# One weighted pass over values and ones in the log attention, with picking matmuls and a re-cut order of the steps

## The chip, the cores and the metric

The kernel runs on one core of a Trainium2 chip. The metric is the time of one execution on the device in microseconds; lower is better. An interval between two kernels comes from runs of both on the same chip.

## What is computed

The input is x, 8 batches of 512 tokens with 128 features, all float32. Four layers follow each other, each added to x after a layer norm: a linear attention, a mixture of 8 experts with a shared one (two chosen per token), the *log attention*, and the mixture of experts again. The change touches the log attention:

```
qkv = x @ w_qkv.T ; k_y = x @ w_ky.T            # 16 heads of 8 dims
L   = q.k  * scale ; L_y = q.k_y * scale         # 512 x 512 per head
agg = sum(exp(clip(L_y, -15, 15)) * mask, -1) + EPS
r   = log(abs(L) + eps) - log(agg + eps)
w   = softplus(r) * mask
A   = w / (sum(w, -1) + EPS)
out = (A @ v) @ w_proj.T
```

So there are two passes over the scores of a batch. *A* makes exps of L_y and sums them. *B* makes the weights w and needs, for each query, the sum of w times the values (8 numbers a head, the numerators) and the sum of w (one number a head).

## The kernel before

Everything is written out by hand: each engine has its own program, and semaphores join them. In the log attention the work goes in steps. `tensor_step`, `scalar_step`, `vector_step` and `pool_step` are called for n = 0 to 99 (and early, for negative n, from inside the first experts' layer by `TENSOR_LEAD`, `VECTOR_LEAD`, `SCALAR_LEAD`). A batch has DUS = 10 steps; n = 10a + i, so i is the place in a batch's ten. Step n does the A part of unit n and the B part of unit m = n - 16 (LAG = 6 and ten steps). Steps 0 to 15 have A alone, 16 to 79 both, 80 to 95 B alone, and from 80 on the second experts' layer is led in (`lead_tensor`, `lead_vector`, `lead_pool`).

`PIECES` says what unit i covers: one or two (s, kb, column, q0, width), 512 columns in all, where s is one of four stacks of heads, kb a block of 128 keys and q0 the first query. A unit covers 4 heads (j). Each step has two halves, u = 0 and 1, of two heads each:

- TensorE (PE): `scores` of half 0 (L1735), `sum_exps` (L1767, exps of unit n - 2 times `ones_s` into bank 4), `weight_values(.., 5)` (L1783, weights of unit m - 2 times `values` into bank 5), `scores` of half 1, `weight_values(.., 6)` (L1783 too, the same weights times `ones_s` into bank 6), then one extra of the batch's ten.
- VectorE (DVE): `abs_scores` half 0 (L2001, out of PSUM), `clip_exps` of the last step's half 1 (L1993), `abs_scores` half 1, extras, `clip_exps` half 0, extras.
- ScalarE (ACT): `exponential` half 0 (L1875), `logarithm` (L1881), extras, `exponential` half 1, `logarithm`, extras.
- GpSimd (POOL): the masks (L2112), and indirect DMAs of the experts' layers around it.

A's scores have banks 0 and 1, B's have 2 and 3, in steps 16 to 79. So half 1 of `scores` can start when exp and abs of half 0 have read these banks, and the next half 0 when those of half 1 have.

A weights matrix of 32 columns for stack s has values in 8 columns (8s to 8s+7) and zeros elsewhere, so the four stacks add up side by side in one bank. The ones matrices are built alike.

The extras of a batch on PE, each at a step's end: `project` q again for r (q2, i = 0), `project_out` (1), `turn` (2), `project` q, ky, k (3, 4, 5), `project_v` (6), `sum_prefix` in three parts (7 to 9). All of them use bank 7, one after the other in the order of `SHARED_BANK`: each waits until ACT or DVE has read the one before. On DVE `empty` (L2045, L2046) reads banks 6 and 5 at i = 8, `correct` (L2035, L2036) makes two corrections at i = 9, `divide` (L2051) follows at 9, `split_low` (L2008) makes low parts of q, ky, k at 4 to 6. `add_choice` (L1483) adds results of the first experts' layer at i = 0 and 1 of a ten, up to a = 5, so in four of the tens within steps 16 to 79. ACT makes the high parts (`split_high`, L1891) and `copy_v` (L1902), and inverts with Ln and Exp.

Below are the functions that the diff touches.

## Time and profile before

| | us |
|---|---|
| median of 3 runs | 1060.55 (1060.13 to 1067.85) |
| the profiled execution | 1063.56 |
| its span, first to last instruction | 1061.8 |
| PE busy | 855.8 |
| DVE busy | 732.6 |
| ACT busy | 566.2 |
| POOL busy | 569.9 |

A span is one execution seen by the profiler; what lies outside it (1.8 us) is the launch and the end. Busy is the union of an engine's instructions; matmuls overlap each other, so a busy PE need not be at its peak. One fp32 matmul of the program makes two records of PE. In the rows, PEld is the weight load of PE; `x_res` rows named in the log attention are `r_buf` and `d_buf`, `w_a` is `q_scaled`, `y_out` is `delta_v` and `delta_n`, `ring_a` is the exps and `ring_b` the weights.

### The profile page before, as it was taken

The page shows a single profiled execution, that of the slowest core. Times are in us where ns is not written, and L with a number is a line of the kernel's source. Part 1 is how long each engine was busy: PE and PEld are TensorE (multiplying, and loading weights), DVE is VectorE, ACT ScalarE, POOL GpSimd, SP SyncE. Part 2 cuts the span into 40 slices and gives each one's busy share as a digit, 9 for nine tenths or more (in the row PEclk, how much of TensorE's full clock was granted, in tenths as well). Part 3 has the DMA queues.
Part 4 walks back from the last instruction along what each step waited for, and adds up shares of the span by engine and source line. Part 5 has one row for each costly group of instructions (what it writes and reads, how often), then busy time and mean ns, then how long its engine had stood idle before and what let it go on. Part 6 is the DMA issues. An engine that isn't in the chain of part 4 may idle for free.

```text
span 1061.8 us, 21386 instructions
## 1 busy us (share of the span) xinstructions
PE 855.8 (81%) x7419; PEld 571.3 (54%) x7419; DVE 732.6 (69%) x1538; ACT 566.2 (53%) x797; POOL 569.9 (54%) x774
## 2 busy tenths in 40 slices
PE   4887577899986778888888888888888767899890
PEld 2676466799872333333333333343444346799890
DVE  3888746465654578797978787778878835465574
ACT  2454242233345778797878788778773332233230
POOL 2343685870655565556533333334324887788784
PEclk9999688999996899999999999999987788999896
DMA  9970012142355766555637363732210021132444
GB/s 298 271 103 1 20 40 70 61 129 81 98 150 157 215 188 186 160 153 151 190 103 197 88 207 93 209 87 77 80 41 11 31 78 40 39 91 81 137 124 128
DMA packets 114120, 123.85 MB, mean 117 GB/s; under 512 B 13296, under 2 KB 76272, under 8 KB 113888
## 3 DMA queue, kind: packets, MB, share of 16 engines
q1 hardware_dynamic: 96224, 100.54, 34.1%
q0 software_dynamic: 8416, 17.29, 5.2%
q10 hardware_dynamic: 9376, 4.65, 1.5%
q8 instruction: 63, 1.03, 0.4%
q14 instruction: 41, 0.34, 0.1%
HBM read 59.71 MB, written 62.72 MB: 115 GB/s over the span
## 4 chain that ended last, share of the span: by engine, by line
PE 41%; DVE 17%; issue 14%; POOL 13%; ACT 6%; DMA 5%; SPq 2%; POOLq 0%; DVEq 0%; ACTq 0%
PE psum L1783 7%; PE psum L1735 6%; DVE ring_b L2001 5%; PE psum L1767 5%; PE psum L828 4%; POOL y_token L1065 4%; POOL pause_room L486 3%; POOL x_sorted L1041 3%; PE psum L1801 2%; PE psum L842 2%; PE psum L780 2%; DVE parts L2008 2%; PE psum L791 2%; PE psum L751 2%; PE psum L1816 1%
## 5 line engine op out<-in xcount | busy, mean ns | idle before, releaser
L2001 DVE TENSOR_SCALAR ring_b<-psum 128x1024 int32<-128x1024 int32 x160 | 195.0, 1222 | 71.7 <-PE psum L1735 71.3
L1875 ACT ACTIVATE ring_a<-psum 128x1024 f32<-128x1024 f32 x160 | 163.2, 1024 | 88.3 <-PE psum L1735 82.2
L2112 POOL TENSOR_SCALAR_AFFINE_SELECT ring_b<-ring_b 128x512 f32<-128x512 f32 (+1 forms) x112 | 84.6, 770 | 215.3 <-ACT ring_b L1881 215.1
L1881 ACT ACTIVATE ring_b<-ring_b 128x1024 f32<-128x1024 f32 x160 | 168.3, 1053 | 41.0 <-DVE ring_b L2001 40.6
L1735 PE MATMUL psum<-stacks 32*128 32x128 f32 (+3 forms) x1024 | 102.9, 387 | 40.4 <-DVE ring_b L2001 22.0
L1993 DVE TENSOR_SCALAR ring_a<-ring_a 128x1024 f32<-128x1024 f32 x160 | 120.4, 757 | 21.5 <-ACT ring_a L1875 21.4
L1735 PEld LDWEIGHTS psum<-stacks 32*128 32x128 f32 x1024 | 59.4, 193 | 132.2 <-issue 73.3
L943 ACT ACTIVATE ring_b<-psum 128x512 f32<-128x512 f32 x72 | 42.6, 591 | 111.5 <-PE psum L828 79.5
L1783 PE MATMUL psum<-ring_b,values 128*32 128x256 f32 (+3 forms) x1024 | 91.5, 467 | 9.1 <-POOL ring_b L2112 5.6
L2112 POOL TENSOR_SCALAR_AFFINE_SELECT ring_a<-ring_a 128x512 f32<-128x512 f32 (+1 forms) x112 | 81.1, 737 | 27.9 <-DVE ring_a L1993 27.9
L1767 PE MATMUL psum<-ring_a,ones_s 128*32 128x256 f32 (+3 forms) x1024 | 93.2, 474 | 2.5 <-POOL ring_a L2112 1.5
L1086 POOL DMA_INDIRECT r_rows<-y_sorted,rows_of x64 | 68.8, 1075 | 48.8 <-issue 41.7
L842 PE MATMUL psum<-w_expert,ring_b 128*128 x568 | 85.3, 285 | 11.9 <-ACT y_out L959 7.0
L1439 DVE TENSOR_TENSOR ring_b<-psum,ring_b 128x512 f32<-128x512 f32 x72 | 49.2, 684 | 64.0 <-ACT ring_b L943 51.3
L1783 PE MATMUL psum<-ring_b,ones_s 128*32 128x256 f32 (+3 forms) x1024 | 91.2, 464 | 0.0
L842 PEld LDWEIGHTS psum<-w_expert,ring_b 128*128 128x128 f32 x568 | 72.8, 194 | 19.0 <-issue 18.9
L1065 POOL DMA_INDIRECT y_token<-y_out,token_of x71 | 70.9, 998 | 22.0 <-POOL pause_room L486 18.7
L1041 POOL DMA_INDIRECT x_sorted<-r_rows,rows_of x64 | 63.8, 996 | 31.3 <-POOL pause_room L486 15.3
L486 POOL MEMSET pause_room<- 128x256 f32 x220 | 75.9, 345 | 0.2
L1041 POOL DMA_INDIRECT x_marked<-r_rows,rows_of x64 | 63.8, 997 | 20.9 <-POOL pause_room L486 16.0
L828 PE MATMUL psum<-ring_a,ring_b 128*128 128x128 f32 x576 | 72.0, 279 | 3.5 <-issue 1.9
L828 PEld LDWEIGHTS psum<-ring_a,ring_b 128*128 128x128 f32 x576 | 69.0, 196 | 4.9 <-issue 3.0
(211 smaller groups left out, 1492.0 us busy)
## 6 DMA issues: line engine op xcount, KB each, us to landing
stack_q<-parts SPq DMA_DIRECT2D x32, 256.0 KB
stack_ky<-parts SPq DMA_DIRECT2D x32, 256.0 KB
stacks<-stack_q SPq DMA_DIRECT2D x64, 128.0 KB
stacks<-stack_ky SPq DMA_DIRECT2D x64, 128.0 KB
stack_k<-parts SPq DMA_DIRECT2D x32, 256.0 KB
stacks<-stack_k SPq DMA_DIRECT2D x64, 128.0 KB
stack_qr<-parts SPq DMA_DIRECT2D x32, 256.0 KB
stacks<-stack_qr SPq DMA_DIRECT2D x64, 128.0 KB
```

The costliest lines, as they stand in the source:

```text
L828: mm = nc.tensor.matmul(bank(2 * (k % 2) + g)[:, at:at + 128], w_pages[i % 4][:, g * INNER + c * 128:g * INNER + (c + 1) * 128], x_turned[ ...
L842: mm = nc.tensor.matmul(tiles(bank(4))[:, i % 4, :], hidden[:, self.items.index(("pair", j)) % 8, at:at + 128], w["w_expert"][:, bass.ds(s ...
L1041: nc.gpsimd.indirect_dma_start(out=out, out_offset=bass.IndirectOffsetOnAxis(ap=rows_of[:, n, at + t:at + t + 1], axis=0), in_=row, in_off ...
L1065: nc.gpsimd.indirect_dma_start(out=y_token, out_offset=bass.IndirectOffsetOnAxis(ap=token_of[:, n, s:s + 1], axis=0), in_=y_out[:, n % 2, ...
L1735: mm = nc.tensor.matmul(bank(2 * pair + j % 2)[:, column:column + width], keys[rows, s, kb * 128:(kb + 1) * 128], queries[rows, s, q0:q0 + ...
L1767: mm = nc.tensor.matmul(psum[32 * j:32 * j + 32, 4, q0:q0 + width], ones_s[:, s, :], exps[:, n % RING, j, column:column + width], start=i ...
L1783: mm = nc.tensor.matmul(psum[32 * j:32 * j + 32, into, q0:q0 + width], weight, ring[:, m % RING, j, column:column + width], start=i == 0, ...
L1875: nc.scalar.activation(exps[:, n % RING, 2 * u:2 * u + 2, :], psum[:, first:first + 2, :], ACT.Exp, scale=SCALE).then_inc(self.exp, 1)
L1881: nc.scalar.activation(part, part, ACT.Ln, bias=1.0).then_inc(self.ln, 1)
L1993: nc.vector.tensor_scalar(part, part, CLIP_LO, CLIP_HI, ALU.max, ALU.min).then_inc(self.clip, 1)
L2001: nc.vector.tensor_scalar(ring[:, m % RING, HEADS_B[u][0]:HEADS_B[u][1] + 1, :].bitcast(I32), psum[:, first:first + 2, :].bitcast(I32), 0x ...
L2112: ins = nc.gpsimd.affine_select(out=part, in_=part, pattern=[[0, part.ap[1][1]], [1, 128]], compare_op=ALU.is_ge, fill=0.0, base=0, channe ...
```

## The change

1. **One pass.** A weights matrix now has, for two neighbouring stacks, 16 columns each: 8 of values and 8 of ones. `weight_values` runs once a unit. Units 0 to 4 of a batch (stacks 0 and 1) add into bank 5, units 5 to 9 (stacks 2 and 3) into bank 6; `PIECES` is re-ordered for that. POOL writes the ones once, beside the memset of the values' room.
2. **Picks.** Numerators and sums now lie mixed in two banks. ACT copies bank 5 out (`evict_first`, i = 3), DVE bank 6 (`evict_second`, i = 8), and TensorE picks them apart by four fp32 matmuls of 128x512 a batch with 0/1 matrices: sums at i = 8 and 9, numerators at i = 0 of the next ten (for the last batch all four at once, at i = 8 and 9). `take_sums` and `take_numerators` read them from bank 6 in place of `empty`.
3. **Order.** The extras of PE now stand at two places of a step, after `sum_exps` and after `weight_values`, and neighbours use different banks: q2 and the picks bank 6, v and ky bank 5, the rest bank 7. DVE's and ACT's extras are placed anew too.

```diff
+    column = np.arange(D)
+    group, stack, dim = column // 32, column // HD % GROUPS, column % HD
+    for name, shift in (("pick_numerators", 0), ("pick_sums", HD)):
+        pick = np.zeros((128, 2, D))
+        pick[32 * group + 2 * HD * (stack % 2) + shift + dim, stack // 2, column] = 1
...
-        VECTOR_LEAD = {0: (-12,), 4: (-6,), 5: (-5,), 6: (-4, -7), 9: (-2,)}
-        TENSOR_LEAD = {3: (-8,), 4: (-7,), 5: (-6,), 6: (-5,)}
+        VECTOR_LEAD = {0: (-12,), 4: (-6,), 5: (-5,), 6: (-4, -3), 9: (-2,)}
+        TENSOR_LEAD = {3: (-7,), 4: (-6,), 5: (-5,), 6: (-4,)}
...
+                    ones = bass.AP(values, HD, [values[:].ap[0], [2 * OW, 2 * TT * HALF], [OW + 2 * HD, 2], [1, HD]])
+                    nc.gpsimd.memset(ones, 1.0).then_inc(set_values, 1)
...
+        BANK_OF = {"q2": 6, "v": 5, "ky": 5, "y": 7, "turn": 7, "q": 7, "k": 7, "prefix": 7}
...
-            def weight_values(self, pe, m, into):
+            def weight_values(self, pe, m):
...
+                pe.wait_ge(self.mask_b, m + 1)
+                if i == 0:
+                    pe.wait_ge(self.v_ready, b + 1)
+                    pe.wait_ge(self.first_out, b)
+                    pe.wait_ge(self.v_tok, min(b + 2, B))
...
+                if i == HALF_DONE:
+                    pe.wait_ge(self.emptied, 2 * b)
+                    pe.wait_ge(self.q_ready, min(b + 2, B))
+                into = 5 if i < HALF_DONE else 6
...
+            def pick(self, pe, b, n, a):
+
+                if n == 0 and a == 0:
+                    pe.wait_ge(self.first_out, b + 1)
+                    pe.wait_ge(self.second_out, b + 1)
+                if n == 1 and a == 0:
+                    pe.wait_ge(self.emptied, 2 * b + 1)
+                mm = nc.tensor.matmul(bank(6), picks[n][:, a, :], evicted[a], start=a == 0, stop=a == 1, skip_group_check=True)
...
                 self.scores(pe, n, m, 0)
                 if 0 <= n - 2 < STEPS_A:
                     self.sum_exps(pe, n - 2)
...
+                if i == 0 and 0 <= a - 3 < B - 1:
+                    self.pick(pe, a - 3, 1, 0)
+                if i == 2 and 0 <= a - 3 < B - 1:
+                    self.project_out(pe, a - 3)
+                if i == 3 and a + 1 < B:
+                    self.turn(pe, a + 1)
+                if i in (4, 5, 6) and a + 1 < B:
+                    self.project(pe, ("q", "ky", "k")[i - 4], a + 1)
+                if i in (7, 8) and 0 <= a - 1 < B:
+                    self.sum_prefix(pe, a - 1, ((0,), (2,))[i - 7])
+                if i == 9 and 0 <= a - 2 < B:
+                    if last:
+                        self.pick(pe, a - 2, 1, 0)
+                    self.pick(pe, a - 2, int(last), 1)
...
                 self.scores(pe, n, m, 1)
...
+                    self.weight_values(pe, m - 2)
+                if i == 0 and 0 <= a - 3 < B - 1:
+                    self.pick(pe, a - 3, 1, 1)
+                if i == 1 and 0 <= a - 1 < B:
                     self.project(pe, "q2", a - 1)
...
+                if i == 3 and 0 <= a < B:
                     self.project_v(pe, a)
...
+                if i == 8 and 0 <= a - 2 < B:
+                    self.pick(pe, a - 2, 0, 0)
+                    if last:
+                        self.pick(pe, a - 2, 0, 1)
...
+            def evict_first(self, a, b):
+                a.wait_ge(self.weighted, DUS * b + HALF_DONE)
...
+                nc.scalar.copy(evicted[0], bank(5)).then_inc(self.first_out, 1)
...
+            def evict_second(self, v, b):
                 v.wait_ge(self.weighted, DUS * (b + 1))
+                v.wait_ge(self.q_ready, min(b + 2, B))
+                nc.vector.tensor_copy(evicted[1], bank(6)).then_inc(self.second_out, 1)
```

In `scalar_step`, `invert_sums` goes to the end of i = 1, `finish_delta` to i = 8, `invert_weights` from i = 8 to i = 0 of the next ten (for the last batch it stays), `evict_first` and `copy_v` stand at i = 3 and 4 ahead of `exponential` half 1, and `split_high` behind it. In `vector_step`, `scale_q` goes from the end of i = 1 into i = 2, `add_output` from 2 to 3, `add_choice` from 0 and 1 to 4 and 5, the statistics from 3 to 7, the corrections to 0 and 1 of the next ten, and most extras stand between the two halves. `pool_step`'s rstd goes from 4 to 8.

PE, a middle step of a batch (i = 5), before: two halves of scores, the exps' sums, values, ones, and the projection k at the end.

```order
L1735 MATMUL psum<-stacks 128x256 x2
L1735 MATMUL psum<-stacks 128x512 x2
L1735 MATMUL psum<-stacks 128x256 x2
L1767 MATMUL psum<-ring_a,ones_s 32x384 x4
L1767 MATMUL psum<-ring_a,ones_s 32x128 x4
L1783 MATMUL psum<-ring_b,values 32x512 x4
L1735 MATMUL psum<-stacks 128x256 x2
L1735 MATMUL psum<-stacks 128x512 x2
L1735 MATMUL psum<-stacks 128x256 x2
L1783 MATMUL psum<-ring_b,ones_s 32x512 x4
L1801 MATMUL psum<-o_tok,b_k 128x512
```

The same step of PE now (L1762 is the scores, L1794 the exps' sums, L1815 the weights times values and ones, L1844 a projection):

```order
L1762 MATMUL psum<-stacks 128x512 x4
L1794 MATMUL psum<-ring_a,ones_s 32x384 x4
L1794 MATMUL psum<-ring_a,ones_s 32x128 x4
L1844 MATMUL psum<-o_tok,b_ky 128x512
L1762 MATMUL psum<-stacks 128x512 x4
L1815 MATMUL psum<-ring_b,values 32x256 x8
```

One pass of 512 columns by four heads is gone from the second half, and the projection (ky now) stands in the first.

PE at the end of a batch's B part now, i = 8 second half to i = 9 (L1828 is a pick, L1859 `sum_prefix`):

```order
L1762 MATMUL psum<-stacks 128x512 x2
L1762 MATMUL psum<-stacks 128x384 x2
L1762 MATMUL psum<-stacks 128x128 x2
L1794 MATMUL psum<-ring_a,ones_s 32x256 x8
L1828 MATMUL psum<-x_res,pick_sums 128x512
L1762 MATMUL psum<-stacks 128x512 x2
L1762 MATMUL psum<-stacks 128x384 x2
L1762 MATMUL psum<-stacks 128x128 x2
L1815 MATMUL psum<-ring_b,values 32x384 x4
L1815 MATMUL psum<-ring_b,values 32x128 x4
L1859 MATMUL psum<-reaches,v_tok 128x128
```

A pick stands where nothing but the values' pass stood before, in the first half of step i = 9; the last part of `sum_prefix` stays at its end.

DVE from `empty` in i = 8 to `divide` in i = 9, before (the corrections L2035 and L2036 follow right behind it):

```order
L2045 TENSOR_TENSOR x_res<-psum,y_out 128x512
L2046 TENSOR_TENSOR oT<-psum,y_out 128x512
L1993 TENSOR_SCALAR ring_a<-ring_a 128x1024
L2001 TENSOR_SCALAR ring_b<-psum 128x1024
L2027 COPY values<-v_tok 128x4x4x8 x4
L1987 SCALAR_TENSOR_TENSOR nbias<-mean_var,rstd 128x4
L1993 TENSOR_SCALAR ring_a<-ring_a 128x1024
L2001 TENSOR_SCALAR ring_b<-psum 128x1024
L1993 TENSOR_SCALAR ring_a<-ring_a 128x1024
L2001 TENSOR_SCALAR ring_b<-psum 128x1024
L1993 TENSOR_SCALAR ring_a<-ring_a 128x1024
L2051 TENSOR_TENSOR oT<-oT,x_res 128x512
```

and now, over both steps (L2067 abs, L2059 clip, L2115 `evict_second`, L2095 `copy_values`, L2123 `take_sums`):

```order
L2067 TENSOR_SCALAR ring_b<-psum 128x1024
L2059 TENSOR_SCALAR ring_a<-ring_a 128x1024
L2115 COPY x_res<-psum 128x512
L2067 TENSOR_SCALAR ring_b<-psum 128x1024
L2095 COPY values<-v_tok 128x8x2x8 x4
L2053 SCALAR_TENSOR_TENSOR nbias<-mean_var,rstd 128x4
L2059 TENSOR_SCALAR ring_a<-ring_a 128x1024
L2067 TENSOR_SCALAR ring_b<-psum 128x1024
L2059 TENSOR_SCALAR ring_a<-ring_a 128x1024
L2067 TENSOR_SCALAR ring_b<-psum 128x1024
L2123 TENSOR_TENSOR x_res<-psum,y_out 128x512
L2059 TENSOR_SCALAR ring_a<-ring_a 128x1024
```

Three operations of 512 columns and two corrections stood in these two steps, now two in all do; the others moved into the next ten.

## Rows read from the trace of the kernel before

**Rows 1.** Page, part 1: busy us (share of span) xinstructions of each engine.

```profile
PE 855.8 (81%) x7419; PEld 571.3 (54%) x7419; DVE 732.6 (69%) x1538; ACT 566.2 (53%) x797; POOL 569.9 (54%) x774
```

**Rows 2.** Windows: length, then busy and count of PE, PEld, DVE, ACT, POOL; clock; DMA; GB/s.

```profile
383.70:749.20 365.50, 309.88 (x3462) 138.91 (x3462) 300.17 (x422) 296.84 (x352) 162.38 (x210) 0.97 0.50 146
749.20:814.30 65.10, 54.88 (x447) 27.30 (x443) 52.42 (x140) 40.93 (x66) 17.31 (x22) 0.87 0.17 49
814.60:938.30 123.70, 97.97 (x659) 72.59 (x659) 75.56 (x182) 39.40 (x58) 98.96 (x150) 0.85 0.16 50
```

**Rows 3.** Groups of 400 to 800 us: count, busy, mean ns of one, idle before, releaser.

```profile
L2001 DVE TENSOR_SCALAR ring_b<-psum 128x1024 int32<-128x1024 int32 x139 | 169.8, 1222 | 65.5 <-PE psum L1735 65.1 <-issue 0.2
L1783 PE MATMUL psum<-ring_b,ones_s 128*32 128x384 f32 (+3 forms) x888 | 76.0, 449 | 0.0
L1783 PE MATMUL psum<-ring_b,values 128*32 128x384 f32 (+3 forms) x888 | 75.4, 448 | 3.5 <-DVE oT L2046 3.5
...
L1801 PE MATMUL psum<-o_tok,b_k 128*128 128x512 f32 x6 | 3.4, 644 | 2.8 <-DVE parts L2008 2.8
...
L2045 DVE TENSOR_TENSOR x_res<-psum,y_out 128x512 f32<-128x512 f32 x6 | 4.1, 681 | 0.0
```

**Rows 4.** Waits of 400 to 800 us: total, times, longest.

```profile
DVE ring_b L2001 <- PE psum L1735: 65.1, 99, 3.0
ACT ring_a L1875 <- PE psum L1735: 59.0, 68, 2.1
```

**Rows 5.** Timeline of one step (i = 5), and its first row a batch later: start, us.

```profile
551.17 0.51 PE L1735 MATMUL psum<-stacks 32*128 32x256 f32 x6
551.61 1.07 PE L1767 MATMUL psum<-ring_a,ones_s 128*32 128x384 f32 x16
551.72 1.23 DVE L2001 TENSOR_SCALAR ring_b<-psum 128x1024 int32<-128x1024 int32 x1 [1.06 <-PE psum L1735]
551.76 1.03 ACT L1875 ACTIVATE ring_a<-psum 128x1024 f32<-128x1024 f32 x1 [1.60 <-PE psum L1735]
...
552.86 0.68 DVE L1993 TENSOR_SCALAR ring_a<-ring_a 128x1024 f32<-128x1024 f32 x1
553.47 0.51 PE L1735 MATMUL psum<-stacks 32*128 32x256 f32 x6
...
554.02 1.23 DVE L2001 TENSOR_SCALAR ring_b<-psum 128x1024 int32<-128x1024 int32 x1 [0.48 <-PE psum L1735]
...
555.90 1.12 PE L1801 MATMUL psum<-o_tok,b_k 128*128 128x512 f32 x2 [0.93 <-DVE parts L2008]
...
610.09 1.23 DVE L2001 TENSOR_SCALAR ring_b<-psum 128x1024 int32<-128x1024 int32 x1 [1.06 <-PE psum L1735]
```

**Rows 6.** Windows around falls of the clock, columns as in rows 2.

```profile
344.00:350.00 6.00, 4.21 (x47) 1.94 (x39) 2.83 (x5) 4.56 (x6) 3.60 (x4) 1.00 0.70 217
...
588.00:592.00 4.00, 2.45 (x16) 2.04 (x14) 2.56 (x7) 3.44 (x5) 0.37 (x1) 0.73 0.00 0
...
776.00:781.00 5.00, 3.00 (x26) 1.73 (x22) 3.18 (x6) 3.49 (x6) 2.23 (x3) 1.00 0.00 0
...
816.00:821.00 5.00, 5.00 (x41) 2.01 (x40) 4.76 (x11) 1.62 (x2) 4.20 (x7) 0.50 0.13 43
```

**Rows 7.** Timeline behind step 89: POOL's sends, a slow pass, the last read, the first scatter.

```profile
814.63 1.07 POOL L1041 DMA_INDIRECT x_marked<-r_rows,rows_of  x1 [2.35 <-DVE rows_of L1375]
...
816.25 1.93 PE L1783 MATMUL psum<-ring_b,values 128*32 128x384 f32 x16
...
856.48 0.69 DVE L2045 TENSOR_TENSOR x_res<-psum,y_out 128x512 f32<-128x512 f32 x1 [5.74 <-PE psum L1783]
...
867.45 1.04 POOL L1023 TENSOR_TENSOR f_rstd<-f_var_eps,neg_half 128x4 f32<-128x4 f32 x1
...
931.91 0.97 POOL L1065 DMA_INDIRECT y_token<-y_out,token_of  x1 [0.28 <-POOL pause_room L486]
```

More of the change, by code:

```diff
@@ L1615, in build @@
         delta = sb("delta", [128, T])
+        evicted = q_scaled, r_buf[:]
+        picks = [const[k][:].rearrange("p (a n) -> p a n", a=2) for k in ("pick_sums", "pick_numerators")]
         delta_v, delta_n = (y_out[:, k].rearrange("p s n -> p (s n)") for k in range(2))
@@ L1780, in weight_values @@
                 for s, kb, column, q0, width in PIECES[i]:
                     for j in range(4):
-                        weight = values[:, b % 2, kb, 4 * j + s, :] if into == 5 else ones_s[:, s, :]
-                        mm = nc.tensor.matmul(psum[32 * j:32 * j + 32, into, q0:q0 + width], weight,
-                                              ring[:, m % RING, j, column:column + width], start=i == 0,
-                                              stop=i == DUS - 1, skip_group_check=True, tile_position=(0, 32 * j))
@@ L1786, in weight_values @@
-                if into == 6:
-                    mm.then_inc(self.weighted, 1)
+                        mm = nc.tensor.matmul(psum[32 * j:32 * j + 32, into, q0:q0 + width], values[:, b % 2, kb, 4 * j + s, :],
+                                              ring[:, m % RING, j, column:column + width], start=FULL.get(i) == into,
+                                              stop=i in (HALF_DONE - 1, DUS - 1), skip_group_check=True,
+                                              tile_position=(0, 32 * j))
@@ L1890, in split_high @@
                     self.wait_made(a, name, b)
-                nc.scalar.copy(parts[:, u % 2, 0, :], q_scaled[:] if name == "qr" else bank(7)).then_inc(self.high, 1)
+                nc.scalar.copy(parts[:, u % 2, 0, :], q_scaled[:] if name == "qr" else bank(BANK_OF[name])).then_inc(self.high, 1)
             def copy_xT(self, a, b):
@@ L1958, in scalar_step @@
                 if i == 1 and 0 <= a - 1 < B:
+                    self.invert_sums(a_, a - 1)
+                if i == 8 and 0 <= a - 1 < B:
                     self.finish_delta(a_, a - 1)
-                if i == 8 and 0 <= a - 2 < B:
+                if i == 8 and a - 2 == B - 1:
                     self.invert_weights(a_, a - 2)
@@ L2020, in copy_values @@
                 if b == 0:
[L2021 removed]
+                    v.wait_ge(set_values, 2)
                 if b > 1:
@@ L2063, in vector_step @@
                     self.following.lead_logits(v, n - STEPS_A)
-                if i == 8 and 0 <= a - 2 < B:
-                    self.empty(v, a - 2)
                 if 0 <= n - 1 < STEPS_A:
                     self.clip_exps(v, n - 1, 1)
+                if i == 0 and 0 <= a - 2 < B:
+                    self.correct_counts(v, a - 2)
+                if i == 1 and 0 <= a - 3 < B - 1:
+                    self.take_numerators(v, a - 3)
+                if i == 2 and 0 <= a - 1 < B:
+                    self.scale_q(v, a - 1)
@@ new lines, in vector_step @@
+                if i == 3 and 0 <= a - 3 < B - 1:
+                    self.add_output(v, a - 3)
+                if i in (4, 5) and self.previous.first_in_rest - 1 <= self.previous.first_in_rest - 1 + a <= B:
+                    self.previous.add_choice(v, self.previous.first_in_rest - 1 + a, i - 4)
+                if i == 7 and 0 <= a + 2 < B:
+                    self.vector_stats(v, a + 2)
+                if i == 8 and 0 <= a - 2 < B:
+                    self.evict_second(v, a - 2)
+                if i == 9 and last:
+                    self.take_numerators(v, a - 2)
@@ L2068, in vector_step @@
                 if in_b:
                     self.abs_scores(v, m, 1)
+                if i == 1 and 0 <= a - 2 < B:
+                    self.correct_values(v, a - 2)
+                if i == 1 and 0 <= a - 3 < B - 1:
+                    self.divide(v, a - 3)
+                if i == 2 and 0 <= a - 1 < B:
+                    self.split_low(v, "qr", a - 1)
+                if i in (4, 5, 6) and 0 <= a + 1 < B:
+                    self.split_low(v, ("q", "ky", "k")[i - 4], a + 1)
+                if i == 7 and 0 <= a + 2 < B:
+                    self.vector_variance(v, a + 2)
@@ L2070, in vector_step @@
                 if i == 8 and 0 <= a < B:
                     self.copy_values(v, a)
-                if i == 2 and 0 <= a - 1 < B:
-                    self.split_low(v, "qr", a - 1)
-                if i == 2 and 0 <= a - 3 < B:
-                    self.add_output(v, a - 3)
-                if i in (4, 5, 6) and 0 <= a + 1 < B:
-                    self.split_low(v, ("q", "ky", "k")[i - 4], a + 1)
                 if i == 8 and 0 <= a + 2 < B:
                     self.vector_bias(v, a + 2)
+                if i == 8 and last or i == 9 and 0 <= a - 2 < B - 1:
+                    self.take_sums(v, a - 2)
```

167 lines of the change are left out of this document (90 added, 77 removed), and 4 rows, old and new, of the table PIECES.

## The prediction

> **What bounds the kernel now.** I read the page first, then windows by stage, then in the stage of the change the groups, the waits and one step of the timeline, and last what follows the stage.
>
> The page [rows 1] has PE busiest, and no engine is full. So the question is what ends last in each stage, and the windows cut the stages [rows 2]. From 383.7 to 749.2 us both passes run: 64 steps (16 to 79) in 365.5 us, 5.71 us a step. Per step PE is busy 309.88/64 = 4.84 us, DVE 300.17/64 = 4.69, ACT 296.84/64 = 4.64. Three engines lie within 4% of each other and each has about 1 us a step of nothing to do. That is the picture of a ring of hand-overs, not of one full engine. The waits say which way it turns [rows 4]: in 400 us DVE waited 65.1 us for the scores of PE and ACT 59.0 us; the timeline of a step shows why [rows 5]. Scores of half 0 at 551.17 (0.51 us), exps' sums at 551.61 (1.07), then the values' pass, and only then the scores of half 1 at 553.47: 2.30 us behind the first, though DVE had the first ones read 1.14 us after 551.72. Then the ones' pass and the projection at 555.90, and the next scores at about 557.0 (555.90 + 1.12). Here DVE had begun its second abs at 554.02; it stood idle 1.06 us ahead of the same step's first abs and 0.48 ahead of the second. PE is late in both halves. So in this stage a pass less on PE is worth something, as long as PE stays the late one.
>
> From 749.2 to 814.3 steps run beside the lead of the experts, at a granted clock of 0.87 [rows 2]. From 814.63 POOL sends rows, and its sends run on without a gap into the scatters at 931.91 [rows 7]; POOL is busy 98.96 of 123.7 us there [rows 2], pauses included. From 814.6 on the end of the kernel hangs on when POOL begins, and a faster PE gives nothing.
>
> **What is removed on PE.** The ones' pass: 888 records, 76.0 us in the window of rows 3. A step has 12.8 such records (16 pieces by 4 heads by 2 records over 10 steps), so 888 are 69.4 steps and a step loses 1.10 us.
>
> **What is added on PE.** Four picks a batch, fp32 128x512 like the projections. One projection is two records of 0.644 us that overlap to 1.12 [rows 3, 5]: 4.5 us a batch, 0.45 a step. A pick is not in the trace, but its shape and type are those of L1801, so both ends are near: 0 if it falls in an idle moment, 1.12 if not. I take 1.12. Net PE loses 0.65 us a step: 4.84 to 4.19.
>
> **What is added elsewhere.** DVE: `empty` was two reads of 0.68 us; now there is `evict_second` besides `take_sums` and `take_numerators`, one more of 0.68 [rows 3]: 0.07 a step, 4.76. ACT: one copy of a bank, at most the same 0.68: 4.71. The ones' memset of POOL stands behind another memset long before the stage, once; I cost it at nothing, and about 1 us if POOL has no slack there.
>
> **What becomes late next.** With PE at 4.19, DVE's 4.76 is the highest. Floor of the stage: 64 x 4.76 = 305 us against 365.5, a gain of 61 at most; if only PE's net saving comes out and every idle moment stays, 64 x 0.65 = 42. The other end is zero, since the ring of hand-overs can eat it. To choose I walked the ten steps of a batch. The base of a step on DVE is two abs and two clips; start to start an abs takes 1.14 [rows 5] and a clip about its 0.68, so 3.6 us. In this time PE does two scores and two passes, 2 x (0.51 + 1.07) = 3.2, and one or two extras of up to 1.12. An extra of PE in the first half makes that half 0.51 + 1.07 + 1.12 = 2.7 against DVE's 1.8, and it does not come back in the second half, since scores have one pair of banks for each pass and PE can't run ahead of the reader. So what counts is, per half, the longest engine. Extras of 512 columns at 0.68 each on DVE and ACT:
>
> - i = 0: ACT inverts (two) and normalises, PE has two picks: 5.9. i = 1: `invert_sums` (three on ACT), three on DVE, q2 on PE: 5.7.
> - i = 3: `add_output` stands ahead of `turn`, and `turn` ahead of the scores of half 1, so DVE waits there about 1.3 us: 5.5. i = 8: eviction, four value copies, a pick, `finish_delta`: 5.4.
> - i = 4 and 5: projection in half 0, `split_low` waits for `split_high`, which now follows the exp of half 1, and an `add_choice` of some 1.1 us where there is one: 5.6 each, else 4.6.
> - i = 2, 7: 5.1 each. i = 9: 4.9. i = 6: 4.6.
>
> Sum 53.4 us a batch. Once a batch the clock falls to half for a spell (0.73 in 588 to 592 [rows 6]), about 1 us more: 54.4. Before it is 610.09 - 551.72 = 58.4 [rows 5]. So four batches with `add_choice` gain 4.0 each: 16. The other 24 steps take (365.5 - 4 x 58.4)/24 = 5.50 us now; two `add_choice` less make 52.4 a batch, and the last batch has fewer projections, so 4.95 a step: 24 x 0.55 = 13. Together 29. A walk engine by engine misses waits that cross, so I take 6 off: 23 us of the 42.
>
> **Behind the stage.** In steps 80 to 89 PE loses a pass of 1.07 a step, but the hand-over there goes over ACT, DVE and back with logits and turns between, and PE alone is late only in some of them: 3 us of 10, bounds 0 and 10. Past 814.6 nothing is gained. The attention's end is dearer: before, the last pass is read at 856.48 straight away [rows 7]; now copy out (0.68), two picks (2 x 1.12), read (0.68), and two more picks stand ahead of the experts' matmuls on PE, some 3 to 4 us later. Behind it the statistics of the last batch wait for POOL anyway until 867.45 [rows 7], and this hides most: I take 1 us, bounds 0 and 4.
>
> Sum: 23 + 3 - 1 = 25 us off. The profiled execution is 1063.56 us, 3.0 above the median 1060.55; 1063.56 - 25 = 1038.6, on the median's footing 1035.5.
>
> **The clock, weighed against a rule.** Rows: in 344 to 350 PE was busy 4.21 of 6 us and the clock stayed at 1.00 (2.4 GHz); in 776 to 781 it was busy 3.00 of 5 and the fraction stayed 1.00, with a fall after it; in 588 to 592, busy 2.45 of 4, it fell to 1.2 GHz in part (0.73) [rows 6]. The stage as a whole has 0.97 at 85% busy [rows 2]; the forecast makes that about 4.19/5.35 = 78%. [...] The Trainium skill, page "TensorE: Matmul & The Clock Gate", section "The HAM clock gate (the 'warmup' mystery)", says that the throttled clock is the default and only activity lifts it. By that rule taking matmuls away can slow those that are left; the trace agrees so far as the falls stand where PE paused.
>
> **Rivals.**
>
> A. *The ring keeps its length.* The projections of i = 4 to 7 now stand ahead of the scores of half 1, which DVE and ACT wait for, where before they followed everything; `split_low` waits for a later `split_high`. For it: half 0 with an extra is 2.7 us of PE, longer than the 2.30 between scores now [rows 5]. Against it: the second half falls from about 3.1 (0.51 + 1.07 + 1.12 and the hand-over) to under 2. If each such gain is halved, the stage gives 10 and the rest nothing: 1060.55 - 8 = 1052.
>
> B. *All of PE's saving comes out.* The idle moments stay as they are and go with PE: 42 + 3 - 1 = 44 less, 1017. For it: rows 4 put nearly all waits of DVE and ACT on PE. Against it: DVE and ACT have only 0.95 and 1.0 us a step left, and their extras stand in lumps.
>
> C. *Slower: the clock.* Place: the stage of both passes. A pass takes 1.93 us in a stretch with clock 0.50 [rows 6, 7] against 1.07. PE's 4.19 us a step become 4.19 x 1.8 = 7.5, and with the hand-overs a cold step takes some 7.9 against 5.4. Before and after are equal when the new step is 0.3 to 0.4 slower than 5.35, that is when 15% more of the time is cold: a mean clock under 0.89 where 0.97 is now. With 30% more cold, 64 x (0.30 x 2.5 - 0.36) = 25 us slower: 1085. For it: a fall a batch already, less work on PE. Against it: a cold PE is always busy, which lifts the clock again, and steps stay at 78%.
>
> That the change doesn't do what it says can be left out: the order of the instructions shows the pass gone and the picks in.
>
> **How the numbers follow.** Forecast (1025 to 1047) 0.65; A 0.11; B 0.18; C 0.06. Faster by over 1% (10.6 us, about what a measurement tells from none) are the forecast, B, and the better edge of A: 0.84. Within 1%: the rest of A, 0.10. Slower: C, 0.06. The range goes from B's 1017 to just past A's 1052: 1016 to 1055. The likeliest one's own range is 1025 to 1047.
>
> **What would show each step.** The ones' pass gone from the groups and 64 records of picks at 0.64; PE busy about 310 - 42 = 268 us over the 64 steps; DVE's wait for the scores down from 65.1 to about 40 in 400 us; a batch at 54.4 us between equal abs rows, 50 to 52 in the later ones; the clock of the stage at 0.95 or more; POOL's first send near 788 and from there to the end as long as before, within 2 us. Wrong it would be if a batch stays above 57 us (A), or the mean clock of the stage falls under 0.9 (C), or the time from the first send to the end grows by more than 4 us.

## The result, and the profile after

The kernel after takes 1052.19 us (median of 5 runs, 1050.88 to 1056.77), the kernel before 1063.14 (5 runs, 1060.13 to 1067.85). The ratio is 0.9891 with a 95% interval of 0.985 to 0.9932: about 11 us faster, where 25 were forecast. The forecast's 1035.5 stood on the first three runs of before (1060.55); two more moved that median to 1063.14. The profiled execution took 1056.77 us, 4.6 above its median. A few executions of a kernel are slower as a whole, and the medians, ratios and gains of this text leave those out.

The page's part 1, then windows with the same cuts as [rows 2] (both passes; steps 80 to the first marked send; from there to the first scatter), columns as there:

```profile
PE 832.1 (79%) x6459; PEld 551.6 (52%) x6459; DVE 744.2 (71%) x1546; ACT 569.1 (54%) x805; POOL 566.7 (54%) x775
```

```profile
393.84:740.62 346.78, 286.17 (x2678) 118.78 (x2682) 308.75 (x434) 296.65 (x357) 159.53 (x209) 0.95 0.54 153
740.62:804.45 63.83, 53.94 (x338) 27.51 (x331) 52.86 (x141) 42.99 (x70) 18.43 (x23) 0.81 0.18 50
804.45:925.40 120.95, 89.97 (x545) 64.22 (x544) 74.20 (x182) 38.00 (x56) 93.67 (x142) 0.80 0.14 44
```

The 64 steps (16 to 79) went from 365.5 us to 346.8 (-18.7; forecast -23), the next stretch from 65.4 to 63.8 (-1.6; forecast -3), and from the first send to the end it is 1054.9 - 804.45 = 250.4 us against 247.2 (+3.3; forecast +1). That is -17.0. But step 16 begins at 393.84 where it began at 383.71, and this +10.1 the profile gives back. It is scatter as far as the profiles tell: the first exp of the log attention's scores came between 323.5 and 334.0 us in the 14 profiles of this study, and this profile has the latest; step 16 began at 383.3 to 392.2 us (mean 387.3) in the six profiles with the old order, and at 382.5 to 393.8 (mean 388.7) in the eight with the new one.

Groups of 400 to 800 us, to set beside [rows 3]:

```profile
L2067 DVE TENSOR_SCALAR ring_b<-psum 128x1024 int32<-128x1024 int32 x145 | 176.6, 1219 | 34.8 <-PE psum L1762 34.6
L1828 PE MATMUL psum<-w_a,pick_sums 128*128 128x512 f32 x14 | 7.9, 645 | 0.0
L1492 DVE SCALAR_TENSOR_TENSOR x_res<-r_rows,gate,x_res 128x128 f32<-128x128 f32 x32 | 22.1, 751 | 0.0
```

The waits of the same stretch, beside [rows 4]; the last two lines are from the kernel before:

```profile
ACT ring_a L1927 <- PE psum L1762: 46.0, 55, 2.6
...
PE psum L1762 <- DVE ring_b L2067: 31.7, 41, 2.6
...
PE psum L1735 <- DVE ring_b L2001: 14.1, 21, 1.2
PE psum L1793 <- DVE x_res L2055: 7.3, 4, 2.0
```

The picks cost what was said in this stretch (0.645 us a record). DVE's wait for the scores fell from 65.1 to 34.6 us. The way back grew: PE now waits 31.7 us for DVE to have read the scores, where it waited 14.1. And the group L1492, the additions of the chosen experts' rows, has a mean of 751 ns.

I cut the 64 steps by the start of each step's first abs, into tens from step 16 on. Three tens with choice additions take 57.06, 57.23 and 58.24 us, the two without them 52.1 and 49.7. The first ten has choice additions too and takes 53.9: in it no attention output is there yet to be added, so nothing delays its step 3 (4.6 us). The steps of a middle batch, by place in the batch, against the forecast's walk:

```
step i            0    1    2    3    4    5    6    7    8    9    sum
forecast's walk  5.9  5.7  5.1  5.5  5.6  5.6  4.6  5.1  5.4  4.9  53.4
before           4.9  6.4  6.4  6.8  5.5  5.8  5.9  4.7  5.9  6.1  58.4
after            5.0  5.8  5.7  7.8  6.8  6.7  5.0  4.7  5.4  4.4  57.3
```

Two places differ from the walk: step 3, and steps 4 and 5, with 21.3 us where it has 16.7. The other seven sum to 36.0, where it has 36.7.

Step 3 of a batch in the kernel after: start, us, engine, line, operation.

```profile
542.51 0.68 DVE L2141 TENSOR_TENSOR x_res<-psum,x_res 128x512 f32<-128x512 f32 x1
543.25 0.66 PE L1836 MATMUL psum<-identity,x_hat 128*128 128x128 f32 x4 [2.20 <-DVE x_res L2141]
543.84 0.51 PE L1762 MATMUL psum<-stacks 32*128 32x384 f32 x8
544.43 1.23 DVE L2067 TENSOR_SCALAR ring_b<-psum 128x1024 int32<-128x1024 int32 x1 [1.23 <-PE psum L1762]
...
545.60 2.08 PE L1849 MATMUL psum<-b_v,xT 128*128 128x128 f32 x8
...
548.49 1.23 DVE L2067 TENSOR_SCALAR ring_b<-psum 128x1024 int32<-128x1024 int32 x1 [2.23 <-PE psum L1762]
```

The same in windows, columns as in [rows 2]: the wait of PE, and what follows it.

```profile
541.00:543.20 2.20, 0.05 (x4) 0.00 (x0) 2.19 (x3) 1.83 (x3) 0.78 (x2) 1.00 0.77 231
543.20:547.40 4.20, 4.15 (x28) 2.66 (x28) 1.83 (x2) 2.46 (x3) 1.06 (x2) 0.70 0.56 178
```

The turn (L1836) needs bank 7, which `add_output` (L2141) reads; that stands in DVE's step behind abs and clip, and the turn now stands ahead of the scores of half 1. PE waits 2.20 us, DVE waits 1.23 us for the scores behind it, and in the next 4.2 us the clock is partly at 1.2 GHz (0.70), which this text calls cold. So `project_v` takes 2.08 us where it takes 1.16 in the kernel before, and DVE waits once more, 2.23 us, for the scores of the next step. PE's wait at the turn is not new: the kernel before has it too, four times in 400 to 800 us and 7.3 us in all (L1793 in the waits above).

Steps 4 and 5:

```profile
550.23 2.77 DVE L1492 SCALAR_TENSOR_TENSOR x_res<-r_rows,gate,x_res 128x128 f32<-128x128 f32 x4
550.48 1.09 POOL L2210 TENSOR_SCALAR_AFFINE_SELECT ring_b<-ring_b 128x1024 f32<-128x1024 f32 x1 [6.22 <-ACT ring_b L1933]
550.49 1.23 DVE L1492 SCALAR_TENSOR_TENSOR x_res<-r_rows,gate,x_res 128x128 f32<-128x128 f32 x1
551.53 1.33 POOL L2210 TENSOR_SCALAR_AFFINE_SELECT ring_a<-ring_a 128x512 f32<-128x512 f32 x2
552.92 1.21 DVE L2067 TENSOR_SCALAR ring_b<-psum 128x1024 int32<-128x1024 int32 x1
...
554.39 0.51 PE L1762 MATMUL psum<-stacks 32*128 32x512 f32 x4 [2.49 <-DVE ring_b L2067]
...
556.47 2.08 PE L1844 MATMUL psum<-o_tok,b_ky 128*128 128x512 f32 x2
```

Four additions take 2.77 us here; in the kernel before each took 336 to 347 ns. One of them starts 0.01 us behind a mask of POOL that lasts 1.09, and takes 1.23. The mask keeps its 1.09 us.

I went through all additions of this kind in the 14 profiles, 128 in each. 101 start while a mask of POOL runs, and 100 of these end 0.14 to 0.15 us behind the end of that mask, after 710 to 1232 ns. Of the 1691 others all but three take 330 to 416 ns. It goes the other way too, but by little: a mask that starts while an addition runs takes a median of 1136 ns, not 1091 (128x1024), or 683, not 634 (128x512). The reads of scores, whose input is in PSUM, take 1205 to 1226 ns beside a mask and 1201 to 1226 elsewhere (after and the third experiment below).

### The profile page after: what moved, and what is told of

Same layout as the page of the kernel before. It is cut to its first block and busy times, and to the rows that moved or that the text cites. A ratio compares the mean times of both kernels' runs of the same rounds, so it can differ in the third digit from the quotient of the medians.

```text
span 1054.9 us, 19542 instructions
## 1 busy us (share of the span) xinstructions
PE 832.1 (79%) x6459; PEld 551.6 (52%) x6459; DVE 744.2 (71%) x1546; ACT 569.1 (54%) x805; POOL 566.7 (54%) x775
## 5 line engine op out<-in xcount | busy, mean ns | idle before, releaser
L2067 DVE TENSOR_SCALAR ring_b<-psum 128x1024 int32<-128x1024 int32 x160 | 194.6, 1218 | 35.0 <-PE psum L1762 34.8
L2210 POOL TENSOR_SCALAR_AFFINE_SELECT ring_b<-ring_b 128x512 f32<-128x512 f32 (+1 forms) x112 | 79.3, 721 | 208.5 <-ACT ring_b L1933 208.3
L1762 PE MATMUL psum<-stacks 32*128 32x128 f32 (+3 forms) x1024 | 100.3, 390 | 65.3 <-DVE ring_b L2067 39.7
L1762 PEld LDWEIGHTS psum<-stacks 32*128 32x128 f32 x1024 | 57.6, 196 | 167.5 <-ACT ring_a L1927 77.1
L2059 DVE TENSOR_SCALAR ring_a<-ring_a 128x1024 f32<-128x1024 f32 x160 | 112.4, 708 | 22.5 <-ACT ring_a L1927 22.5
L1794 PE MATMUL psum<-ring_a,ones_s 128*32 128x256 f32 (+3 forms) x1024 | 94.2, 478 | 15.4 <-ACT delta L1972 8.2
L1815 PE MATMUL psum<-ring_b,values 128*32 128x256 f32 (+3 forms) x1024 | 100.0, 503 | 7.4 <-POOL ring_b L2210 7.4
L1047 POOL DMA_INDIRECT x_marked<-r_rows,rows_of x64 | 63.8, 997 | 19.7 <-POOL pause_room L492 16.3
L834 PE MATMUL psum<-ring_a,v_tok 128*128 128x128 f32 x560 | 68.5, 275 | 0.5 <-issue 0.5
```

Of the source, the lines that this page charges most:

```text
L834: mm = nc.tensor.matmul(bank(2 * (k % 2) + g)[:, at:at + 128], w_pages[i % 4][:, g * INNER + c * 128:g * INNER + (c + 1) * 128], x_turned[ ...
L1047: nc.gpsimd.indirect_dma_start(out=out, out_offset=bass.IndirectOffsetOnAxis(ap=rows_of[:, n, at + t:at + t + 1], axis=0), in_=row, in_off ...
L1762: mm = nc.tensor.matmul(bank(2 * pair + j % 2)[:, column:column + width], keys[rows, s, kb * 128:(kb + 1) * 128], queries[rows, s, q0:q0 + ...
L1815: mm = nc.tensor.matmul(psum[32 * j:32 * j + 32, into, q0:q0 + width], values[:, b % 2, kb, 4 * j + s, :], ring[:, m % RING, j, column:col ...
L2059: nc.vector.tensor_scalar(part, part, CLIP_LO, CLIP_HI, ALU.max, ALU.min).then_inc(self.clip, 1)
L2067: nc.vector.tensor_scalar(ring[:, m % RING, HEADS_B[u][0]:HEADS_B[u][1] + 1, :].bitcast(I32), psum[:, first:first + 2, :].bitcast(I32), 0x ...
```

## The experiments

All times are ratios to the kernel before on the same chip; before's medians there were 1063.8 to 1066.0 us. "After" is 0.9891. A ratio is the estimate that belongs to its interval, not the quotient of the two medians; 0.001 of it is 1.06 us. Experiments ran on three chips, so gains between two of them are given by their ratios.

**The choice additions at the end of steps 4 and 5.**

```
-  between the reads:  if i in (4, 5) ...: self.previous.add_choice(...)
+  after clip_exps(v, n, 0):  if i in (4, 5) ...: self.previous.add_choice(...)
```

> The kernel after, with the two choice additions (the four routed rows' multiply-adds of a step, 128x128 each) moved in the same steps 4 and 5 from between the two reads of scores to the end of DVE's step. Theory 1 (they are slow because GpSimd's triangle masks run in that moment on the same memory): each addition falls from about 700 ns (a group of four 2.7 us) back to about 345 ns (1.13 us), the four batches that have them go from about 57.4 us to 54 to 55.5, and the kernel is 8 to 12 us faster than after: 1040 to 1044. Theory 2 (they are slow for another reason, as the rows that the DMA lays beside them, in whatever place): group stays at 2 us or more and the kernel stays within 3 us of 1052. Theory 3 (the batch is long because of the clock's falls, not of the additions): the additions are 1.13 us again but the batch stays at 57, kernel at 1049 to 1054.

Measured: 1047.42 us, ratio 0.9833 (0.9796 to 0.987).

```profile
L1492 DVE SCALAR_TENSOR_TENSOR x_res<-r_rows,gate,x_res x40: 330/344/348, 384.0 to 608.9; 128x128 f32<-128x128 f32 x40
```

Minimum, median and maximum are 330, 344 and 348 ns: the same instructions, away from the masks, are quick again. A batch is 54.8 to 56.6 us (forecast 54 to 55.5). The gain, some 6 us by the ratios (the two intervals overlap a little), is below the 8 expected: steps 4 and 5 are still 6.2 and 5.9; their second half now holds `split_low`, clip and additions, all on DVE.

**The choice additions back at the end of steps 0 and 1.** The same edit with `i in (0, 1)`.

> The kernel after, with the choice additions back where they were before: end of DVE's steps 0 and 1. Theory 1 (GpSimd's masks beside them): additions at about 345 ns, as in the run with them at the end of steps 4 and 5; but steps 0 and 1 are the full ones on DVE and ACT (5.9 and 5.7 us in the forecast's walk), so 1 to 3 us slower than at 4 and 5: 1042 to 1046. Theory 3 (clock): no change from after, 1049 to 1054.

Measured: 1039.87 us, ratio 0.9767 (0.9729 to 0.9805), 13 us less than after. Additions at a median of 340 ns. The place was misjudged: steps 0 and 1 grow only to 5.5 and 6.3, while 4 and 5 fall to 5.2 and 4.7. The 64 steps take 331.6 us against after's 346.8.

**The same move in the kernel before, alone:** from the end of steps 0 and 1 to between the reads.

```
+  before abs_scores(v, m, 1):  if i in (0, 1) ...: self.previous.add_choice(...)
-  after clip_exps(v, n, 0):    if i in (0, 1) ...: self.previous.add_choice(...)
```

> The kernel before, with one part of the change alone: the choice additions of steps 0 and 1 moved from the end of DVE's step to between the two reads of scores, behind the clip that releases GpSimd's masks. Theory 1 (DVE and GpSimd hold each other up there): additions at 600 to 1200 ns instead of 340 to 346, a group of four at 2.3 us or more, and about 1 to 1.6 us more a step, 2 to 3 us in each of four or five batches: 6 to 14 us slower than before, 1069 to 1077. Rival (the additions were slow in after through something of after's own, as its new data or steps): 340 ns each, and the kernel as before within 3 us.

Measured: 1074.57 us, ratio 1.0111 (1.0072 to 1.015).

```profile
L1483 DVE SCALAR_TENSOR_TENSOR x_res<-r_rows,gate,x_res x32: 337/711/1227, 410.4 to 598.6; 128x128 f32<-128x128 f32 x32
```

340 ns became 711 by the place alone, and three batches in a row take 61.4 us where they took 58.3. So the slowness belongs to the moment, not to anything else in after. The Trainium skill, page "SBUF — State Buffer", section "Who interferes with whom", states that a DVE instruction with two SBUF inputs contends with a GpSimd instruction that reads SBUF, and that such contention is an exclusive lock. The addition has two such inputs (r_rows, x_res). The traces agree: 100 of the 101 additions that started beside a mask ended only behind it, and the reads from PSUM were not slowed.

**The output's addition a step earlier**, on top of the additions at steps 0 and 1.

```
-  if i == 3 and 0 <= a - 3 < B - 1: self.add_output(v, a - 3)      # between the reads
+  if i == 2 and 0 <= a - 3 < B - 1: self.add_output(v, a - 3)      # after clip_exps(v, n, 0)
```

> The kernel with the choice additions at the end of steps 0 and 1, and the addition of the attention's output (x_res<-psum,x_res) moved from between the reads of step 3 to the end of step 2. Theory T (step 3 is 7.7 us where the forecast had 5.5, because the turn waits 1.96 us on that addition and stands ahead of the scores of half 1): step 3 falls to 5.5 to 6.3, step 2 grows by 0.3 to 0.6, each batch 1.3 us shorter, 5 to 8 us in all: 1033 to 1036. Rival (step 3 is long through the clock's fall, which comes there anyway): step 3 above 7, time within 2 us of 1041.

Measured: 1030.84 us, ratio 0.9694 (0.9665 to 0.9722), 8 us below the version without it.

```profile
523.98 0.68 DVE L2141 TENSOR_TENSOR x_res<-psum,x_res 128x512 f32<-128x512 f32 x1
...
524.72 0.66 PE L1836 MATMUL psum<-identity,x_hat 128*128 128x128 f32 x4 [0.24 <-DVE x_res L2141]
```

The turn's wait is 0.24 us here, step 3 is 4.6 us where it was 6.2 to 8.7, step 2 grew by 0.6. Four batches in a row take 50.9 to 51.0 us. It gave the most that was expected, since the cold spell behind the turn went as well. The profiles with the new order bear this out: where the turn waited 1.94 to 2.20 us, the clock of the next 4.2 us was below 1.00 in 13 of 20 cases; where it waited 0.23 to 0.47, in none of 12.

**The same alone on the kernel after** (choice additions left between the reads).

> The kernel after, with the output's addition at the end of step 2 alone; the choice additions stay between the reads of steps 4 and 5. If the turn's wait costs by itself: step 3 falls from 7.7 us to about 5, 8 to 11 us faster than after, 1041 to 1044, and the two misses of the forecast are separate and add. If the stalls of steps 4 and 5 hold the ring anyway: 0 to 4 us faster, 1048 to 1052.

Measured: 1043.74 us, ratio 0.9786 (0.9757 to 0.9815): 11 us less than after, the upper end of what was expected for a cost of its own. Steps 4 and 5 stay at 6.7 to 7.3 us in the batches with choices. The two misses are separate, and they nearly add: 0.9891 falls by 0.0105 with this one, by 0.0124 with the other, and by 0.0197 with both, to 0.9694.

**What the ones' pass was worth: put back as zeros.** In the version with the additions at steps 0 and 1, behind each values' pass:

```
+  for s, kb, column, q0, width in PIECES[i]:
+      for j in range(4):
+          mm = nc.tensor.matmul(psum[32 * j:32 * j + 16, into, q0:q0 + width], const["pick_sums"][:, 16:32],
+                                ring[:, m % RING, j, column:column + width], start=False, ...)
```

> The kernel with the choice additions at the end of steps 0 and 1, and behind each values' pass of all steps the same pass again with zero weights: the new order and banks with the old load of PE. It splits the gain of that kernel over before (about 22 us) into its two parts. If the pass is what gives (as forecast: 0.65 us a step of PE): the 64 steps grow from 331.6 us by 25 us or more, back to about 360, kernel 1060 to 1068. If the order gives and the pass's worth is eaten by the clock (as leaving the pass out in the old order, which made it 25 us slower, suggests): the 64 steps stay at 335 to 345 us and the kernel at 1038 to 1052.

Measured: 1048.02 us, ratio 0.985 (0.9818 to 0.9882). The two stretches without and with the zero pass:

```profile
392.33:723.91 331.58, 279.72 (x2694) 117.04 (x2691) 295.78 (x435) 296.99 (x357) 159.35 (x210) 0.97 0.58 160
723.91:793.37 69.46, 59.91 (x337) 30.44 (x329) 53.00 (x141) 42.97 (x70) 18.38 (x24) 0.68 0.15 46
```

```profile
388.40:735.20 346.80, 324.31 (x3482) 135.30 (x3486) 299.17 (x435) 300.06 (x357) 158.65 (x210) 0.99 0.54 154
735.20:799.01 63.81, 57.86 (x469) 29.04 (x471) 53.01 (x140) 42.67 (x70) 17.91 (x24) 0.89 0.17 50
```

A pass of 1.10 us a step is worth 15.2/64 = 0.24 in the 64 steps. In the whole time it is worth 0.985 - 0.9767, some 9 us. Behind the 64 steps this pair of profiles has 5.6 us against the version without the pass, at a clock of 0.68 instead of 0.89, but that version has the coldest such stretch of the five profiles with the new order and no zeros: 63.8 us (0.81), 65.4 (0.82), 66.9 (0.74), 67.5 (0.72) and 69.5 (0.68). With the pass put back it is 63.8 (0.89). With PE's old load and more, the new order alone takes the 64 steps from 365.5 to 346.8. The range that was expected for the second theory was 335 to 345 us, and the kernel came out in its range, 1038 to 1052. So in this version the order gives the larger part (15 of 23 thousandths of the time) and the pass the rest; for after itself nothing was run that splits its 11 us.

**The ones' pass left out in the old order**, so that the denominators and with them the results are wrong, in three ways: pieces 1 to 8, 1 to 4, 5 to 8 of ten (pieces k stand in step k - 2).

```
-  for s, kb, column, q0, width in PIECES[i]:
+  for s, kb, column, q0, width in () if into == 6 and left_out else PIECES[i]:
```

> The kernel before, with the ones' pass left out in eight of a batch's ten steps (kept in the first and the last, so that bank and hand-over stay; the denominators lack the other steps' sums) and nothing else changed: the worth of PE's saving alone in the old order. PE loses 8/10 of 1.10 us a step, 0.88. If all came out: 64 x 0.88 = 56 us, 1004. Forecast's view (the ring gives back about half): 25 to 35 us faster, 1028 to 1038. If the ring keeps its length: 5 to 12 faster, 1051 to 1058.

> The kernel before, with the ones' pass left out for pieces 1 to 4 of ten (they stand in steps 9, 0, 1 and 2 of a batch, where before's clock falls already; the denominators lack these sums). Leaving out eight of ten made the kernel 25 us slower at a mean clock of 0.91 in the 64 steps. Clock theory: these are the steps with the most idle time on PE, so these four make it slower: 1066 to 1085, clock 0.91 to 0.95. Rival (the slower time came from something else than the clock, as from the wrong numbers): no relation to which steps they are; both of this pair alike.

> The kernel before, with the ones' pass left out for pieces 5 to 8 (steps 3 to 6 of a batch, in which PE has a projection each; the denominators lack these sums). Clock theory: PE stays busy there, so the clock holds nearly and the saving shows: 1050 to 1064, clock 0.95 or more. Rival: like the other of the pair.

Measured: 1089.44, 1073.10 and 1089.77 us; ratios 1.0254 (1.0211 to 1.0298), 1.0037 (1.0002 to 1.0072) and 1.0232 (1.0202 to 1.0263). Less work, and slower: clearly in the first and the third, by at most 0.7% in the second, whose profiled execution (1078.77 us) was one of its longer ones. None of the three expectations for the first had it slower. The 64 steps in that order:

```profile
384.90:766.41 381.51, 282.37 (x2776) 129.42 (x2774) 297.52 (x422) 297.62 (x352) 161.49 (x210) 0.91 0.49 139
```

```profile
383.35:755.46 372.11, 295.18 (x3112) 134.21 (x3109) 298.94 (x423) 297.40 (x352) 160.84 (x210) 0.94 0.51 143
```

```profile
392.22:774.29 382.07, 305.85 (x3126) 136.17 (x3124) 297.52 (x423) 297.12 (x352) 162.15 (x210) 0.91 0.48 138
```

The clock is 0.91 to 0.94 where before had 0.97, and steps grow where the pass is missing: with pieces 1 to 4 out, steps 1 and 2 are 7.6 and 6.6 to 8.1 us and steps 4 to 8 as before; with pieces 5 to 8 out, steps 5 and 6 are 7.8 to 8.0 where the clock is down, and step 1 stays at 6.4. Tied to the place as it is, the longer time doesn't come from the changed numbers. My pick of which half would hurt was wrong, though. The timeline with eight pieces out shows why:

```profile
559.83 1.12 PE L1802 MATMUL psum<-o_tok,b_ky 128*128 128x512 f32 x2 [1.94 <-DVE parts L2009]
...
565.61 1.13 PE L1802 MATMUL psum<-o_tok,b_k 128*128 128x512 f32 x2 [1.92 <-DVE parts L2009]
...
571.39 1.46 PE L1807 MATMUL psum<-b_v,xT 128*128 128x128 f32 x8 [1.92 <-DVE parts L2009]
572.78 0.80 PE L1735 MATMUL psum<-stacks 32*128 32x512 f32 x6
573.51 1.94 PE L1767 MATMUL psum<-ring_a,ones_s 128*32 128x256 f32 x16
```

In the old order every projection goes to bank 7 (L1802 and L2009 are L1801 and L2008 of before) and waits until DVE has read the one before. The pass filled that wait: with it PE idled 0.93 us there [rows 5], without it 1.9. The saving turns into waiting, PE pauses longer, and behind the longer pauses all of PE's work runs at half speed for a while (1.94 us for a pass). That the pauses bring the cold spells is read from this order in the trace and from the step 3 cases above; no run changed the clock by itself.

**The zero pass in steps 80 to 97 only**, on the version with the additions at steps 0 and 1: the loop above under `if m >= STEPS_A - DUS - 8`.

> The kernel with the choice additions at the end of steps 0 and 1, and in steps 80 to 97, behind each values' pass, the same pass again with weights that are all zero (it adds zero, and costs PE the 1.07 us that the ones' pass cost). Clock theory: the granted clock of the stretch from step 80 to the first marked send rises from 0.68 to 0.80 or more, and the stretch falls from 69.5 us to 64 to 67: 1036 to 1039. Rival (the clock follows something else, or PE's time is what bounds there): 5 to 10 us longer, 1046 to 1051.

Measured: 1038.23 us, ratio 0.9763 (0.9732 to 0.9794), against 0.9767 without.

```profile
715.61:779.92 64.31, 57.46 (x465) 29.43 (x461) 53.09 (x141) 42.99 (x70) 18.39 (x23) 0.89 0.17 50
```

The stretch is 5.2 us shorter than in the one profile of the version without, at a clock of 0.89, as the clock theory says: PE does 64 matmuls more (128 records) and is done sooner. Beside all five profiles without zeros (63.8 to 69.5 us, mean 66.6) the three with them have 63.8 to 64.7 at 0.89: they take the cold away, but what that is worth lies between nothing and 5.6 us from execution to execution. In the whole time it can't be told from nothing.

**The output's addition early and the zero passes together.**

> The choice additions at the end of steps 0 and 1, the output's addition at the end of step 2, and the zero-weight passes in steps 80 to 97: all three that came out well, together. If they add: the stretch from step 80 to the first marked send falls from 68.7 us (clock 0.83 in that profile) to 64 to 66, the kernel 2 to 4 us below 1030.8: 1026 to 1029. If the clock there is high by itself once the output comes early: within 1.5 us of 1030.8.

Measured: 1030.37 us, ratio 0.9676 (0.9656 to 0.9696), against 1030.84 and 0.9694. The second expectation holds: no difference that these runs tell. The stretch is 64.7 us against 65.4 (0.82) without zeros; the 68.7 of the expectation was cut at a later send than the first, so there was little to gain from the start.

**The picks' tables alone**, loaded in the kernel before and not used: `"pick_numerators": 2 * D, "pick_sums": 2 * D` in its list of constants.

> The kernel before, with the two tables of the picks loaded at the start and used by nothing. In the profiled run of after the log attention began 8 to 10 us later than in before. Theory E1 (the tables' 256 KB of loads at the start shift all that follows): 2 to 8 us slower than before, the first scores of the log attention at 328 to 333 us. Theory E2 (the start of a run scatters by itself, or something else shifts it): same as before within 2 us, first scores within the scatter of the other profiles.

Measured: 1063.65 us, ratio 0.9999 (0.9972 to 1.0026). The loads cost nothing. The late start in after's profile was not theirs.

## Why the prediction was wrong, point by point

- **What bounds: right.** PE was late in both halves, and DVE's wait for it was nearly halved. That the gain would lie in the 64 steps held as well. PE busy there came to 286 us, not the 268 of the forecast; part of it is cold work (a record of the projection ky 976 ns instead of 645).
- **The walk, i = 3: the step that failed first.** "DVE waits there about 1.3 us: 5.5." The wait was about right (1.23 us), but the walk took step 3 as if nothing followed. PE itself stood 2.20 us, the clock fell, `project_v` and the next scores ran cold, and DVE waited again, 2.23 us. Measured 7.8: 2.3 us a batch more than the walk, of which the 1 us kept apart for a cold spell covers less than half. The output moved one step earlier gave 8 us, and 11 on after alone.
- **The walk, i = 4 and 5: the second.** "an `add_choice` of some 1.1 us where there is one". The duration was taken from a place where no mask of POOL runs beside it. Between the reads it stands just behind the clip that releases POOL's masks, and costs 2.7 us: 6.8 instead of 5.6 a step. For the four batches with choices the forecast had 54.4; the three that have both faults took 57.1 to 58.2, the first, which has this one alone, 53.9. For those without choices it had 52.4, and the chip 52.1 and 49.7. Back at steps 0 and 1 it gave 13 us.
- **The worth of the pass: wrong in its reason.** "Net PE loses 0.65 us a step", and a good half of that was to come out. The pass itself gives 0.24 a step in the version with the additions at steps 0 and 1; the larger part of that version's gain is of the new order and banks, which the forecast counted as the cost of getting the pass out. That its sum for the stage was near all the same is in part luck.
- **Six off for waits that cross:** the walk had 336.5 us for the 64 steps, the chip 346.8. The two above are such waits, and they account for more than the six: the three batches that have both took 9.3 us more than 3 x 54.4.
- **Steps 80 to 89:** 1.6 us for 3 forecast; the clock of that stretch, 0.87 before, is 0.81. Of the five profiles of the new order without zeros the coldest have the longest such stretch (67.5 us at 0.72, 69.5 at 0.68), so this is likely what eats it.
- **The tail:** +3.3 us, inside the bounds of 0 and 4, not the 1 taken. Before, POOL came late to the statistics (they were ready at 863.95, it took them at 867.45). Now it waits for them: they are ready at 860.79, and it takes them at 860.93 after 3.82 us of nothing:

```profile
849.74 0.69 DVE L2123 TENSOR_TENSOR x_res<-psum,y_out 128x512 f32<-128x512 f32 x1 [3.93 <-PE psum L1828]
854.30 0.69 DVE L2132 TENSOR_TENSOR oT<-psum,y_out 128x512 f32<-128x512 f32 x1 [3.87 <-PE psum L1828]
...
860.93 1.04 POOL L1029 TENSOR_TENSOR f_rstd<-f_var_eps,neg_half 128x4 f32<-128x4 f32 x1 [3.82 <-issue]
```

  A pair of picks takes 3.8 us there, as the clock is at 0.50. The forecast priced them at 1.12 each. The size of +3.3 is that of one pair of profiles: this stretch takes 244.8 to 252.8 us in the six profiles with the old order (mean 247.3) and 247.3 to 250.5 in the eight with the new one (mean 249.0).
- **The rivals.** A had the right size (1052), and the forecast's own sign for A came: batches above 57 us. The place is right only in part: the turn ahead of the scores of half 1 is one of its kind, the projections are not, since steps 4 and 5 take 5.2 and 4.7 us once the additions have left them, where the walk has 4.6 each. C's mechanism is real: the old order is 25 us slower without the pass. In the new order it doesn't decide: the stage's clock stayed at 0.95, as forecast. A likely reason is that a projection no longer waits for the last one's reader (the five projections ky between 400 and 800 us waited 4.8 us in all for it in before, and 0.0 in after); no run tests that alone. The cold spell behind the turn is C's mechanism too, and it is part of the step that failed.

What stays open: the profiles' stages sum to 17 us of gain, the medians to 11. The interval (7 to 16 us) nearly reaches it. One profile of a kernel is not its median: the 64 steps took 365.5 us in before's profile and 362.6 in that of the same order with the two tables. Also open is what the output's addition, moved a step earlier, would give in the kernel before, whose turn waits as well; it was not run.

## What to carry to other kernels

Before an instruction is moved, look at what the other engines do at its new place, not only at how full its own engine is: here a DVE operation with two inputs in SBUF that started beside a mask of GpSimd lasted until 0.14 us behind the end of that operation. Whatever stands ahead of the scores in a ring's order must not wait for an engine that itself waits for the scores; a reader moved one step earlier was worth 8 to 11 us, where the whole change had given 11. And a pass that only fills a wait gives nothing when it goes, as long as the wait stays: to price work taken off an engine, ask what ends last there without it.

## What was not expected of the hardware

Less work on TensorE made the kernel slower: without 8/10 of a pass, the granted clock of 64 steps fell from 0.97 to 0.91 and they took 381.5 us instead of 365.5. The other way round, 64 further matmuls with zero weights didn't make a stretch longer: 63.8 to 64.7 us in three profiles at 0.89 of full clock, against 63.8 to 69.5 in five without them at 0.68 to 0.82. A DVE addition of 340 ns took up to 1232 ns beside GpSimd's masks of 1.09 us, which themselves took 1.14 at most.
